# Mamba stage: where ScalarE's two silus, one evacuation and the norm's root, and VectorE's first two gates, stand in the loop body

## The chip, the cores and the metric

The kernel runs on one core of one Trainium2 chip, as one launch. The time is device time in microseconds (us) of that core. The program is written by hand for five queues: TensorE (PE), VectorE (DVE), ScalarE (ACT), GpSimd (POOL) and SyncE (SP, which only issues DMAs). Each runs its instructions in the order written, and they meet through semaphores.

## The reference

A chain of four blocks in float32 on x (8 x 512 x 256) and a context (8 x 64 x 192): attention with a feed-forward, a Mamba block, attention with a feed-forward, attention. The change touches the second, of which this is the core:

```
p = silu(prepend_cond @ pre_w1) @ pre_w2
h = concatenate([p, x], axis=1)
for l in range(4):
    h = h + mamba_block(rmsnorm(h, norm_w[l]), ...)

def mamba_block(x, ip_w, cw, cb, xp_w, dtp_w, dtp_b, A_log, Dp, op_w):
    xi, z = split(x @ ip_w.T)                  # 512 channels each
    xi = silu(conv(xi, cw, 4 taps, causal) + cb)
    dt, Bm, Cm = split(xi @ xp_w.T)            # 16, 16, 16
    dt = softplus(dt @ dtp_w.T + dtp_b)
    dA = exp(dt[..., None] * -exp(A_log))      # 512 channels x 16 states
    dBu = dt[..., None] * Bm[:, :, None, :] * xi[..., None]
    h_t = dA_t * h_(t-1) + dBu_t ;  ys_t = sum over states of h_t * C_t
    y = (ys + xi * Dp) * silu(z)
    return y @ op_w.T
```

With 8 batches of 64 + 512 positions there are 4608 positions a layer.

## The kernel before, in words

The Mamba stage (function `mamba`) cuts the 4608 positions of a layer into 9 chunks of 512 (`TC`) and walks layer by layer, chunk by chunk: 36 loop bodies, written out. The 512 channels x 16 states are 64 units of 128 rows (i = 0 to 63), two to a pair (j = i // 2, 0 to 31), and eight pairs to each fourth of the channels (k = j // 8).

For each unit ScalarE makes the decays, `exp(dt * A)`, into one of four banks of PSUM (line 2474); VectorE runs the scan along the 512 positions (line 2429); then the state is multiplied by C. In 22 of 32 pairs VectorE does that product (`times_c`, line 2237), in the ten pairs of `BY_POOL` (0, 5, 8, 11, 14, 16, 20, 24, 26, 28) GpSimd does (line 2511), three pairs behind its own product of u and B (line 2506), which fills a ring of six pairs. TensorE adds up each pair by two times two matmuls with `fold` into a bank for y (line 2384, `summed`). After eight pairs `gate` (line 2232) multiplies that bank by silu(z).

Before ScalarE makes the exponentials of pair j, `slots_free` waits until pair j-2 has left its banks. For a pair of VectorE it waits for the product (`prod_d`) and copies the last state out of the banks (line 2133); for a pair of GpSimd it waits for the scan (`scanned`) and copies from the ring (line 2129).

Between the exponentials the same body prepares the next chunk: the operations that are not the scan's are hung on an index. TensorE's projections stand at pairs, before the pair's own sum: convolution products E0 to E3 (line 1992; the last at pairs 2 and 3), the residual products B1 and B0 (lines 2034 and 2043; pairs 5 and 6), the norm's mean C (line 2018; pair 7), the products for dt, B and C, named G (line 2052; pairs 10 and 11), dt's products H and z's products F. ScalarE's evacuations stand behind the exponential of a unit: for each i, the exponential, then what `late_act` hangs on i, then what `early_act` hangs on i. `E_OUT` holds the units of the four convolution evacuations, `SILU_AT` those of silu of x and silu of z, each over 128 x 2048 with a table load before it and one behind it (lines 2173, 2174 and 2168, 2169). `RESIDUAL` is (19, 18): the evacuation of B0 (line 2143) behind unit 19, of B1 behind 18. `SQUARE_AT` is 5: a copy of three columns (line 2204) and the square (line 2205). `RSTD_AT` holds the logarithm (line 2208) and the exponential (line 2211) of the norm; VectorE applies the result at units 26 and 27 (line 2222). The gates of fourths 0, 1 and 2 stand before the scans 23, 39 and 55; that of fourth 3 before scan 7 of the next body.

The z of a body is given its silu in that body, the x of the next chunk in this one; G waits for the latter. GpSimd forms u = dt * x (`times_x`, line 2252), behind pairs 26 and 31, followed by one small operation (line 2255) which sets dt to a large value where a batch begins in the chunk, and otherwise writes to a scratch column. SyncE copies dt and u to all rows a fourth ahead (lines 2267 and 2274), stores B and C (line 2279), loads them again spread out, and loads the next layer's weights in the last two chunks of a layer.

Of the kernel before, what the change touches and what calls it, by code (L numbers as in the profile page):

```python
# [18 lines left out]
ALU = mybir.AluOpType  # L19
# [1804 lines left out]
def load_first(e, core, layer):  # L1824

    e.dma_start(core.weights[1][:, CONV_AT:CONV_AT + TAPS * KD * DI], layer_of(core.taps, layer)).then_inc(core.first_loaded, 16)
    e.dma_start(layer_vec(core, "norm", "conv_b"), vec_from(core, layer, "norm", "conv_b")).then_inc(core.first_loaded, 16)
# [62 lines left out]
def v_at(N, name):  # L1890

    return BEFORE_V[name] + 1 if N[1] == -2 else val(N, len(LANE_V), V_BASE + LANE_V[name] + 1)
# [17 lines left out]
def mamba(core):  # L1910
    at = 0
    ring, at = core.area(at, RING, 2, TC)
    dt_rep, at = core.area(at, 2, 2, TC)
    u_rep, at = core.area(at, 2, 2, TC)
    x, at = core.area(at, 2, KI, TC)
    z, at = core.area(at, 2, KI, TC)
# [61 lines left out]
    def reset_of(c):  # L1978

        return 64 * (c % CHUNKS) if c % CHUNKS < B else None  # L1980
# [125 lines left out]
            e.wait_ge(y_free, y_free_at(N, "F1"))  # L2106
        e.matmul(ybank[k % 2], diag[:, k, :], xi[:, k, :], start=True, stop=False)

    E_OUT, G_OUT, F_OUT, SILU_AT = (59, 3, 9, 13), 29, (55, 49, 33, 1), (15, 7)
    H_OUT = (37, 45)  # L2110

    def soft_plus(e, N, pair):
# [82 lines left out]
            e.wait_ge(ln.v_full, v_at(N, "F0"))  # L2195
            e.activation(zi[:, 0, :], lane_v, ACT.Copy).then_inc(ln.v_free, 1)

    SQUARE_AT, RSTD_AT, SCALE_AT = 5, (21, 23), 26

    def early_act(e, N, i, c, xe, nb, nb_before):  # L2200

# [45 lines left out]
    def times_x(e, N, pair, xi, c):  # L2247

        e.wait_ge(ln.s_free, s_at(N, ("H0", "H3")[pair]))
        e.wait_ge(ln.v_free, v_at(N, ("H1", "H2")[pair]))  # L2250
        at = slice(2 * pair, 2 * pair + 2)
        e.tensor_tensor(u[:, at, :], dt[:, at, :], xi[:, at, :], ALU.mult).then_inc(u_done, 1)
        e.wait_ge(u_done, u_done_at(N, pair, 1))
        p = reset_of(c)
        e.tensor_tensor(scrap[:, 12:14] if p is None else dt[:, at, p], far, core.one[:, 0:2], ALU.mult).then_inc(u_done, 1)

    def build_diag(e):

# [26 lines left out]
    with core.nc.Block() as block:  # L2285
        @block.sync
        def _(e):
            store_bc(e, (0, -1), 0)
            e.wait_ge(bc_stored, 16)
            for a in range(2):  # L2290
                for q in range(2):
                    load_bc(e, (0, -1), a, q, 0)
            e.wait_ge(u_done, u_done_at((0, -1), 0, 2))
            spread_dt(e, 0)
            spread_u(e, 0)
            for a in range(2, SP_):
                for q in range(2):
                    load_bc(e, (0, -1), a, q, 0)
            e.wait_ge(u_done, KI)
            for l in range(LAYERS // 2):  # L2300
                for j in range(BODIES):
                    N, c = (l, j), j % CHUNKS
                    layer = l * 2 + j // CHUNKS
                    after = (l * 2 + 2) % LAYERS if j >= CHUNKS else l * 2 + 1
                    e.wait_ge(summed, summed_at(previous(N), PAIRS_N - 1))
                    spread_dt(e, 1)
                    spread_u(e, 1)
                    if c == CHUNKS - 1:
                        load_z(e, core, after)
                    e.wait_ge(scanned, scanned_at(N, 15))  # L2310
                    spread_dt(e, 2)
                    spread_u(e, 2)
                    if c == CHUNKS - 2:
                        load_first(e, core, after)
                    store_bc(e, N, (j + 1) % 2)
                    e.wait_ge(scanned, scanned_at(N, 31))
                    spread_dt(e, 3)
                    e.wait_ge(bc_stored, val(N, 16, 32))
                    spread_u(e, 3)
                    if c == 0:  # L2320
                        load_out(e, core, layer)
                    e.wait_ge(u_done, u_done_at(N, 0, 2))
                    spread_u(e, 0)
                    e.wait_ge(scanned, scanned_at(N, 47))
                    spread_dt(e, 0)
                    if c == CHUNKS - 2:
                        load_middle(e, core, after)
                    for a in range(SP_):
                        pair = 3 * SP_ + a
                        if by_pool(pair):  # L2330
                            e.wait_ge(prod_q, prod_q_at(N, pair))
                        else:
                            e.wait_ge(prod_d, prod_d_at(N, pair))
                        load_bc(e, N, a, 0, (j + 1) % 2)
                        load_bc(e, N, a, 1, (j + 1) % 2)
            for a in range(SP_ // 2):
                e.wait_ge(bc_ready[a], 64 * (STEPS + 1))
            e.wait_ge(rep_in[0], 128 * (2 * STEPS + 1))
            e.wait_ge(rep_in[1], 128 * 2 * STEPS)
            e.wait_ge(core.first_loaded, FIRST_LOAD * (LAYERS + 1))  # L2340
            e.wait_ge(core.z_loaded, Z_LOAD * (LAYERS + 1))
            e.wait_ge(core.middle_loaded, MIDDLE_LOAD * (LAYERS + 1))
            e.wait_ge(core.out_loaded, OUT_LOAD * (LAYERS + 1))
# [49 lines left out]
        @block.vector  # L2393
        def _(e):
            e.memset(state, 0.0).then_inc(set_up, 1)
            e.memset(scrap[:, 18:22], 0.0)
            e.memset(far, FAR).then_inc(set_up, 1)
            e.memset(tiny, TINY).then_inc(set_up, 1)
            e.tensor_tensor(fold, core.ident[:, 0:64], core.ident[:, 64:128], ALU.add).then_inc(set_up, 1)
            e.memset(scrap[:, 1:2], 0.0).then_inc(prod_d, 1)  # L2400
            e.memset(scrap[:, 2:3], 0.0).then_inc(prod_d, 1)
            e.memset(scrap[:, 3:4], 0.0).then_inc(gated, 1)
            for i in range(RING - 1):
                e.memset(scrap[:, 4 + i:5 + i], 0.0).then_inc(summed, 1)
            e.wait_ge(core.first_loaded, FIRST_LOAD)
            for i in range(UN):
                early_dve(e, (0, -2), i, -2, normed[:, 0])
            for i in range(UN):
                early_dve(e, (0, -1), i, -1, normed[:, 1])
            for l in range(LAYERS // 2):  # L2410
                for n in range(BODIES):
                    N, c = (l, n), n % CHUNKS
                    layer = l * 2 + n // CHUNKS
                    for i in range(UN):
                        j, h = i // 2, i % 2
                        k, a = j // SP_, j % SP_
                        if c == CHUNKS - 2 and i == SCALE_AT:
                            e.wait_ge(core.first_loaded, layer * FIRST_LOAD + 2 * FIRST_LOAD)
                        early_dve(e, N, i, c, normed[:, n % 2])
                        for f in range(KI - 1):  # L2420
                            if i == 16 * (f + 1) + 7:
                                gate(e, N, f, z[:, n % 2])
                        if i == 7:
                            gate(e, previous(N), KI - 1, z[:, (n + 1) % 2])
                        if h == 0:
                            e.wait_ge(fed, fed_at(N, j))
                        e.wait_ge(da_full, da_full_at(N, i))
                        da, ub = banks[:, slot_of(i), :], ring_pair(n, j)[:, h, :]
                        e.tensor_tensor_scan(ub if by_pool(j) else da, da, ub, state[:, i:i + 1], ALU.mult, ALU.add).then_inc(scanned, 1)  # L2429
                        if h == 0 and j > 0 and not by_pool(j - 1):  # L2430
                            e.wait_ge(scanned, scanned_at(N, i - 1))
                            times_c(e, N, n, j - 1, 1)
                        if h == 1 and not by_pool(j):
                            e.wait_ge(scanned, scanned_at(N, i - 1))
                            times_c(e, N, n, j, 0)
                        if h == 1 and j == PAIRS_N - 1 and not by_pool(j):
                            e.wait_ge(scanned, scanned_at(N, i))
                            times_c(e, N, n, j, 1)
            N = (LAYERS // 2, 0)
            gate(e, previous(N), KI - 1, z[:, (BODIES - 1) % 2])  # L2440
            for m in range(KD):
                e.wait_ge((ln.s_full, ln.v_full)[m], (s_at(previous(N), "E2"), v_at(previous(N), "E1"))[m] + 1)
                xc = chunk(CHUNKS - 1)[:, m, :]
                e.tensor_tensor(xc, xc, lanes[1 - m], ALU.add)
# [384 lines left out]
```

## Time and profile before

| | us |
|---|---|
| median of 3 runs | 6636.77 |
| lowest and highest run | 6634.72, 6638.04 |
| the profiled execution, its own time | 6639.8 |
| its span | 6638.0 |
| VectorE busy over the span | 4928.1 |
| GpSimd busy over the span | 4394.1 |

The span is the time from the first to the last instruction that the profiler recorded; all times in rows are counted from its start. The mean granted clock of TensorE was 0.941 of its full speed. A row of a timeline is an instruction, or several of one kind behind each other (x2); the bracket at its end is the time for which its engine had stood idle before it, and what ended that. PE rows are matmuls, PEld rows weight loads. The Mamba stage's scans run from 2054.0 to 5992.7 us.

### The profile page before, as it was taken

Reading aid. Unit: us, or ns where it says so; the run is one execution under the profiler, and the core shown is the slowest. Engines: PE = TensorE matmul, PEld = TensorE weight load, DVE = VectorE, ACT = ScalarE, POOL = GpSimd, SP = SyncE. Lnnn points to the kernel's source line nnn. Section 1 sums busy time; section 2 is a strip of 40 time slices with the busy share of each in tenths; the row PEclk is TensorE's granted clock in tenths of the full one; section 3 lists DMA queues with packets and bytes.
Section 4 is the critical chain, followed back from the end, with each engine's and each line's share of the span. In section 5 each row is a group of like instructions: output and inputs, shape, how many; then the busy total and the mean of one; then the engine's idle time right before and its main releaser. Section 6 shows DMA issues by size and latency. Waiting matters only on the chain. (4 is left out here: it accounts for less than half of the span.)

```text
span 6638.0 us, 60681 instructions
## 1 busy us (share of the span) xinstructions
PE 6129.0 (92%) x20586; PEld 2577.4 (39%) x20586; DVE 4928.1 (74%) x5709; ACT 3620.5 (55%) x6605; POOL 4394.1 (66%) x2056
## 2 busy tenths in 40 slices
PE   9999999999999989898899989898989898988898
PEld 4555555544443333323333323333323343323444
DVE  4444445543225999999999999999999999995623
ACT  4444445432225666666666666666666666664432
POOL 3333334323005999999999999999999999992300
PEclk9999999999998989899989999999999898989998
DMA  2000000213002333333333333332333232332000
GB/s 80 1 1 1 1 1 1 86 26 102 20 0 68 83 76 78 78 93 85 72 89 71 83 88 86 71 89 65 89 81 93 65 89 65 93 80 56 4 0 26
DMA packets 228678, 387.64 MB, mean 58 GB/s; under 512 B 46304, under 2 KB 64416, under 8 KB 225936
## 3 DMA queue, kind: packets, MB, share of 16 engines
q1 hardware_dynamic: 228368, 383.75, 23.7%
q8 instruction: 164, 2.69, 0.2%
q14 instruction: 146, 1.20, 0.1%
HBM read 207.14 MB, written 23.40 MB: 35 GB/s over the span
## 5 line engine op out<-in xcount | busy, mean ns | idle before, releaser
L2506 POOL TENSOR_TENSOR work<-work,weights 128x1024 f32<-128x1024 f32 x1152 | 2685.6, 2361 | 15.8 <-PE banks L2384 6.8
L2429 DVE TENSOR_TENSOR_SCAN banks<-banks,work 128x512 f32<-128x512 f32 x1584 | 1985.7, 1272 | 53.5 <-ACT banks L2474 48.1
L2384 PE MATMUL banks<-work 128*64 128x512 f32 x4608 | 1353.9, 670 | 378.2 <-POOL work L2511 271.1
L2474 ACT ACTIVATE banks<-work 128x512 f32<-128x512 f32 x2304 | 1496.0, 680 | 25.5
L1992 PE MATMUL banks<-work,weights 128*128 128x512 f32 (+31 forms) x3796 | 1140.6, 451 | 3.0 <-DVE work L2222 3.0
L2237 DVE TENSOR_TENSOR work<-banks,weights 128x512 f32<-128x512 f32 x1584 | 1056.0, 668 | 0.0
L2511 POOL TENSOR_TENSOR work<-work,weights 128x1024 f32<-128x1024 f32 x360 | 848.0, 2356 | 238.4 <-ACT work L2129 238.4
L2429 DVE TENSOR_TENSOR_SCAN work<-banks,work 128x512 f32<-128x512 f32 x720 | 911.2, 1269 | 99.8 <-ACT banks L2474 97.2
L603 POOL TENSOR_TENSOR work<-work 128x1024 f32<-128x1024 f32 x256 | 479.6, 1893 | 743.4 <-DVE work L470 742.9
L1992 PEld LDWEIGHTS banks<-work,weights 128*128 128x128 f32 x3796 | 634.4, 190 | 600.0 <-issue 523.6
L2133 ACT ACTIVATE work<-banks 128x2 f32<-128x2 f32 x792 | 135.9, 172 | 1227.4 <-DVE work L2237 1225.6
L2384 PEld LDWEIGHTS banks<-work 128*64 128x64 f32 x4608 | 271.0, 145 | 1236.4 <-issue 500.8
L553 ACT ACTIVATE work<-banks,work 128x512 f32<-128x512 f32 x512 | 347.7, 690 | 201.1 <-DVE work L464 201.1
L464 DVE TENSOR_REDUCE work<-banks 128x2 f32<-128x1024 f32 x256 | 308.8, 1214 | 105.1 <-PE banks L389 104.7
L2010 PE MATMUL banks<-work,weights 128*128 128x512 f32 x592 | 350.7, 722 | 0.0
L1040 PE MATMUL banks<-work,weights 128*128 128x512 f32 x768 | 341.5, 599 | 9.4 <-ACT work L215 9.4
L454 DVE COPY work<-banks 128x512 f32<-128x512 f32 x256 | 175.5, 685 | 160.3 <-PE banks L379 160.3
L379 PE MATMUL banks<-ident,work 128*128 128x128 f32 x2048 | 277.9, 279 | 8.2 <-DVE work L454 4.6
L379 PEld LDWEIGHTS banks<-ident,work 128*128 128x128 f32 x2048 | 222.1, 141 | 151.7 <-issue 111.1
L389 PE MATMUL banks<-work 64*128 64x512 f32 x1024 | 254.4, 615 | 0.0
L366 PE MATMUL banks<-work 128*64 128x256 f32 x2048 | 247.5, 385 | 0.0
L322 PE MATMUL banks<-work,weights 128*128 128x512 f32 x512 | 224.9, 597 | 6.4 <-ACT work L215 4.2
(312 smaller groups left out, 6796.9 us busy)
## 6 DMA issues: line engine op xcount, KB each, us to landing
weights<-mamba_bc SPq DMA_DIRECT2D x592, 256.0 KB, 5.0
work<-work SPq DMA_DIRECT2D x1160, 128.0 KB, 2.3
weights<-mamba_taps SPq DMA_DIRECT2D x5, 2048.0 KB, 7.5
weights<-cross_vo SPq DMA_DIRECT2D x16, 512.0 KB, 6.9
mamba_taps<-work SPq DMA_DIRECT2D x4, 2048.0 KB, 7.8
cross_vo<-weights SPq DMA_DIRECT2D x6, 1024.0 KB, 8.4
work<-in_conv_rows SPq DMA_DIRECT2D x16, 256.0 KB, 6.7
out_T<-X SPq DMA_DIRECT2D x8, 512.0 KB, 3.3
```

Source lines behind the costliest of these rows:

```text
L379: mm = e.transpose(core.banks[:, 4 + j, kt * P:(kt + 1) * P], probs[:, 2 * (g % 2) + u, j, kt * P:(kt + 1) * P], core.ident[:])
L553: last = e.activation(probs[:, slot, j, :], core.banks[:, 2 * u + j, :], ACT.Exp, bias=nmax[:, slot, j:j + 1], accum_out=sums[:, slot, j:j ...
L603: e.tensor_tensor(probs[:, slot], probs[:, slot], rsum[:, slot, :].unsqueeze(2).to_broadcast([P, 2, T]), ALU.mult) \
L1040: mm = e.matmul(bank(i), w1[:, k, m * P:(m + 1) * P], normed[:, k, :], start=(k == 0), stop=(k == KD - 1))
L1992: mm = e.matmul(lane[:, a:b], conv_w[j][:, k, m * P:(m + 1) * P], nb[:, k, a + j:b + j], start=(d == 0 and k == 0), stop=(j == 0 and b == ...
L2010: mm = e.matmul(lane, z_w[:, k, m * P:(m + 1) * P], nb[:, k, TAPS - 1:], start=(k == 0), stop=(k == KD - 1))
L2237: last = e.tensor_tensor(ring_pair(n, j)[:, h, :], banks[:, slot_of(i), :], bc[:, j % SP_, 1, :], ALU.mult)
L2384: mm = e.matmul(ybank[k % 2][64 * h:64 * h + 64, :], fold, ring_pair(n, j)[:, h, :], start=False, stop=(a == SP_ - 1))
L2429: e.tensor_tensor_scan(ub if by_pool(j) else da, da, ub, state[:, i:i + 1], ALU.mult, ALU.add).then_inc(scanned, 1)
L2474: e.activation(banks[:, slot_of(i), :], dt_rep[:, k % 2, h, :], ACT.Exp, scale=decay[:, f:f + 1]).then_inc(da_full, 1)
L2506: e.tensor_tensor(ring_pair(n, j), u_rep[:, k % 2], bc[:, a, 0, :].unsqueeze(1).to_broadcast([P, 2, TC]), ALU.mult) \
L2511: e.tensor_tensor(ring_pair(n, q), ring_pair(n, q), bc[:, q % SP_, 1, :].unsqueeze(1).to_broadcast([P, 2, TC]), ALU.mult) \
```

## The change

Four indices move, one small operation and one semaphore step of GpSimd go, and SyncE gets a wait.

- `E_OUT[3]`: the last convolution evacuation stands behind unit 15 in place of 13.
- `SILU_AT`: silu of x behind unit 21 (pair 10) in place of 15, silu of z behind unit 5 (pair 2) in place of 7. At unit 5 `late_act`, with the silu, comes ahead of `early_act`, with the square.
- `RSTD_AT`: logarithm and exponential behind units 23 and 24 in place of 21 and 23.
- `GATE_AT`: the first two gates before scans 21 and 37 in place of 23 and 39; the third stays at 55.
- `times_x`: in a chunk in which no batch begins (the last of each layer) the second operation is left out, and the first counts for two.
- SyncE waits for the last convolution evacuation before it loads the next layer's folded convolution weights.

```diff
--- before.py
+++ after.py
@@ -2106,7 +2106,9 @@
             e.wait_ge(y_free, y_free_at(N, "F1"))
         e.matmul(ybank[k % 2], diag[:, k, :], xi[:, k, :], start=True, stop=False)
 
-    E_OUT, G_OUT, F_OUT, SILU_AT = (59, 3, 9, 13), 29, (55, 49, 33, 1), (15, 7)
+    E_OUT, G_OUT, F_OUT = (59, 3, 9, 15), 29, (55, 49, 33, 1)
+    SILU_AT = (21, 5)
+    GATE_AT = (21, 37, 55)
     H_OUT = (37, 45)
 
     def soft_plus(e, N, pair):
@@ -2195,7 +2197,7 @@
             e.wait_ge(ln.v_full, v_at(N, "F0"))
             e.activation(zi[:, 0, :], lane_v, ACT.Copy).then_inc(ln.v_free, 1)
 
-    SQUARE_AT, RSTD_AT, SCALE_AT = 5, (21, 23), 26
+    SQUARE_AT, RSTD_AT, SCALE_AT = 5, (23, 24), 26
 
     def early_act(e, N, i, c, xe, nb, nb_before):
 
@@ -2249,10 +2251,12 @@
         e.wait_ge(ln.s_free, s_at(N, ("H0", "H3")[pair]))
         e.wait_ge(ln.v_free, v_at(N, ("H1", "H2")[pair]))
         at = slice(2 * pair, 2 * pair + 2)
-        e.tensor_tensor(u[:, at, :], dt[:, at, :], xi[:, at, :], ALU.mult).then_inc(u_done, 1)
+        p = reset_of(c)
+        e.tensor_tensor(u[:, at, :], dt[:, at, :], xi[:, at, :], ALU.mult).then_inc(u_done, 2 if p is None else 1)
+        if p is None:
+            return
         e.wait_ge(u_done, u_done_at(N, pair, 1))
-        p = reset_of(c)
-        e.tensor_tensor(scrap[:, 12:14] if p is None else dt[:, at, p], far, core.one[:, 0:2], ALU.mult).then_inc(u_done, 1)
+        e.tensor_tensor(dt[:, at, p], far, core.one[:, 0:2], ALU.mult).then_inc(u_done, 1)
 
     def build_diag(e):
 
@@ -2311,6 +2315,7 @@
                     spread_dt(e, 2)
                     spread_u(e, 2)
                     if c == CHUNKS - 2:
+                        e.wait_ge(ln.v_free, v_at(N, "E3"))
                         load_first(e, core, after)
                     store_bc(e, N, (j + 1) % 2)
                     e.wait_ge(scanned, scanned_at(N, 31))
@@ -2418,7 +2423,7 @@
                             e.wait_ge(core.first_loaded, layer * FIRST_LOAD + 2 * FIRST_LOAD)
                         early_dve(e, N, i, c, normed[:, n % 2])
                         for f in range(KI - 1):
-                            if i == 16 * (f + 1) + 7:
+                            if i == GATE_AT[f]:
                                 gate(e, N, f, z[:, n % 2])
                         if i == 7:
                             gate(e, previous(N), KI - 1, z[:, (n + 1) % 2])
```

## Rows read from the trace of the kernel before

**Rows 1.** The page: busy table (us, share of the span); ScalarE's exponentials (busy us, mean ns of one).

```profile
PE 6129.0 (92%) x20586; PEld 2577.4 (39%) x20586; DVE 4928.1 (74%) x5709; ACT 3620.5 (55%) x6605; POOL 4394.1 (66%) x2056
...
L2474 ACT ACTIVATE banks<-work 128x512 f32<-128x512 f32 x2304 | 1496.0, 680 | 25.5
```

**Rows 2.** Waits of 2000 to 6200 us: who waited for whom, us, times, longest.

```profile
POOL work L2511 <- ACT work L2129: 238.4, 145, 7.1
...
DVE work L2429 <- ACT banks L2474: 97.2, 37, 25.8
...
DVE banks L2429 <- ACT banks L2474: 48.1, 41, 6.4
...
ACT X L2143 <- PE banks L2043: 16.2, 36, 0.5
DVE work L2232 <- PE banks L2384: 16.2, 8, 12.1
```

**Rows 3.** Windows: PE, PEld, DVE, ACT, POOL busy us (x), PEclk, DMA, GB/s.

```profile
3482.11:3591.08 108.97, 99.46 (x306) 38.17 (x305) 105.79 (x115) 70.39 (x127) 102.41 (x47) 0.91 0.34 78
3482.11:3514.00 31.89, 31.89 (x113) 15.16 (x111) 28.83 (x32) 24.35 (x38) 27.72 (x12) 1.00 0.40 89
3536.00:3544.00 8.00, 7.97 (x16) 1.90 (x18) 8.00 (x10) 6.10 (x10) 8.00 (x4) 0.61 0.60 131
```

**Rows 4.** Timeline of VectorE, one body: start, us, engine, line, op, out<-in [idle].

```profile
3479.94 2.44 DVE L2429 TENSOR_TENSOR_SCAN work<-banks,work 128x512 f32<-128x512 f32 x2
...
3488.80 1.27 DVE L2429 TENSOR_TENSOR_SCAN banks<-banks,work 128x512 f32<-128x512 f32 x1
...
3494.17 1.29 DVE L2429 TENSOR_TENSOR_SCAN banks<-banks,work 128x512 f32<-128x512 f32 x1 [1.14 <-ACT banks L2474]
...
3509.20 1.28 DVE L2429 TENSOR_TENSOR_SCAN work<-banks,work 128x512 f32<-128x512 f32 x1 [1.92 <-ACT banks L2474]
...
3518.66 1.27 DVE L2429 TENSOR_TENSOR_SCAN work<-banks,work 128x512 f32<-128x512 f32 x1
3519.85 0.66 DVE L2237 TENSOR_TENSOR work<-banks,weights 128x512 f32<-128x512 f32 x1
3520.43 0.68 DVE L2232 TENSOR_TENSOR work<-banks,work 128x512 f32<-128x512 f32 x1
3521.03 1.27 DVE L2429 TENSOR_TENSOR_SCAN work<-banks,work 128x512 f32<-128x512 f32 x1
...
3545.53 1.29 DVE L2429 TENSOR_TENSOR_SCAN banks<-banks,work 128x512 f32<-128x512 f32 x1
```

**Rows 5.** Timeline of ScalarE in the same body.

```profile
3484.10 1.04 ACT L2205 ACTIVATE work<-X 128x1024 f32<-128x1024 f32 x1
3487.13 0.17 ACT L2133 ACTIVATE work<-banks 128x2 f32<-128x2 f32 x1 [2.00 <-DVE work L2237]
...
3488.66 1.28 ACT L2168 ACT_TABLE_LOAD   x1
...
3493.17 0.17 ACT L2133 ACTIVATE work<-banks 128x2 f32<-128x2 f32 x1
3493.38 1.30 ACT L2474 ACTIVATE banks<-work 128x512 f32<-128x512 f32 x2
...
3513.54 0.60 ACT L2143 ACTIVATE X<-banks 128x512 f32<-128x512 f32 x1 [0.46 <-PE banks L2043]
...
3514.13 1.29 ACT L2474 ACTIVATE banks<-work 128x512 f32<-128x512 f32 x2
```

**Rows 6.** Timeline of TensorE in the same body.

```profile
3509.91 3.60 PE L2043 MATMUL banks<-work,weights 128*128 128x512 f32 x8
...
3516.36 1.08 PE L2384 MATMUL banks<-work 128*64 128x512 f32 x4
...
3540.00 1.98 PE L2384 MATMUL banks<-work 128*64 128x512 f32 x4
```

**Rows 7.** The GpSimd operation of line 2255: ns min/median/max, first and last start.

```profile
L2255 POOL TENSOR_TENSOR work<-work,one x74: 196/197/198, 2038.7 to 5992.3; 128x2 f32<-128x2 f32 x74
```

## The prediction

> **What bounds the kernel now.** I read, in this order, the busy table of the page, the waits over the Mamba stage, one body of that stage in the windows, and then that body instruction by instruction on VectorE, ScalarE, TensorE and GpSimd. The busy table puts TensorE first [rows 1], but that is a mean over eight stages, and the change touches only the Mamba stage. There the loop body runs 36 times, and one body takes 108.97 us, in which VectorE is busy 105.79, GpSimd 102.41, TensorE 99.46 and ScalarE 70.39 [rows 3]. VectorE, with its 64 scans and 44 products by C, is therefore the bound, and it is idle for only 3.2 us a body. The waits say where: scans wait for ScalarE's exponentials, 97.2 + 48.1 us in all [rows 2], of which one wait of 25.8 is the prologue's. The gates lost only 16.2 us to TensorE over the whole stage, 12.1 of them in one wait at the end. GpSimd's 238.4 us are spent waiting for copies of the state, which come behind VectorE's own scans: slack, not a bound.
>
> In the body read here the idle time of VectorE is two waits: 1.14 us before scan 8, and 1.92 us before scan 16 [rows 4]. Each follows a silu on ScalarE. A silu costs a table load, the activation and a second load: from 3488.66 to 3493.17, that is 4.51 us [rows 5]. The exponentials run at most two pairs ahead, since four banks hold them, so such a block is hidden only if ScalarE's lead is long enough. The next op of VectorE follows a scan after 1.19 us and a product or gate after 0.59 (scan 22, product, gate and scan 23 at 3518.66, 3519.85, 3520.43 and 3521.03) [rows 4]. Without its waits, scan 8 would have started 1.22 earlier and scan 16 2.00 earlier; with about 0.13 before scan 38 [rows 4] the body loses 3.35 us, or 120 us in 36 bodies. That is all that any new order on ScalarE could win.
>
> All times below are of the body whose first scan is at 3479.9, in the span's clock. I carry the new order through it with these durations: copy to first exponential 0.20, one exponential 0.68 [rows 1], a pair of them 1.30, and 0.11 from its end to the scan that waited for it (3493.17, 3493.38 + 0.68, 3494.17) [rows 4, 5].
>
> **Silu of z behind pair 2 (i = 5).** At i = 5 ScalarE is free at 3484.0; what stood there was the square, a small copy and 1.04 us [rows 5]. Pair 3 could start at 3487.13, when its slot came free, so ScalarE had 3 us left over, of which the square took 1.1. Now the silu goes ahead of the square in the same step: 3484.05 + 4.53 = 3488.58, square to 3489.7, copy, exponential 6 done at 3489.7 + 0.20 + 0.68 = 3490.6, scan 6 at 3490.7. It started at 3488.80 before [rows 4]: 1.90 us lost in place of 1.22. By scan 8 VectorE is 0.68 behind the old time. The silu has not become hidden; it has met the square.
>
> **The convolution's last evacuation at i = 15, silu of x no longer there.** The evacuation behind exponential 15 costs no one anything: the next user of its lane is the mean product, much later, and the exponentials 16 and 17 wait for a slot anyway. With no silu, scan 16 goes at the old 3509.20 - 2.00 + 0.68 = 3507.9. VectorE is now 1.3 us ahead of the old time. This is the whole gain, and it stands for about four scans.
>
> **What is late next: TensorE's residual product.** At i = 19 ScalarE evacuates the product of line 2043. Its eight matmuls run from 3509.91 to 3513.51, and ScalarE waited 0.46 for them at 3513.54 [rows 5, 6]; it did so 36 times for 16.2 us [rows 2], so in every body. TensorE is busy without a gap from the body's start to here, 31.89 of 31.89 us at clock 1.00 [rows 3], so this product can't come sooner because VectorE does: its time is fixed to the body's start. ScalarE, 1.3 us earlier at i = 19, only waits longer. It takes up pair 10 at 3514.03 as before and its exponentials at 3514.13 [rows 5]; the first is done at 3514.81 and scan 20 starts at 3514.92. VectorE would have been ready at 3513.8 (from scan 16 four scans at 1.19 and two products at 0.59: 5.9). That is a new wait of 1.1 us, and the gain is spent: the old scan 20 stood two scans and two products, 3.56, ahead of scan 22's 3518.66 [rows 4], at 3515.1.
>
> **Silu of x behind pair 10 (i = 21).** The exponentials 20 and 21 end at 3515.42. The silu follows, to 3519.95; copy and exponential 22: 3519.95 + 0.20 + 0.68 + 0.11 = scan 22 at 3520.94. Before, it started at 3518.66 [rows 4]. **The gate moved to i = 21** stands ahead of scan 21 and needs pair 7's sum, whose four matmuls end at 3517.44 [rows 6]: it waits some 0.7 us, scan 21 starts at 3518.1 and scan 22 could start at 3519.9. So this wait lies wholly under the one for the exponential. The gate that stood before scan 23 is gone there; scan 23 starts at 3520.94 + 1.19 + 0.59 = 3522.72, where it was 3521.03 [rows 4]: **1.69 us late**, and from there on everything that follows VectorE is late by as much.
>
> **The rest.** The logarithm and exponential of the norm at i = 23 and 24 lie in ScalarE's slack: exponential 24 is done at 3523.7 for a scan that can start at 3523.9, exponential 25 at 3524.8 for one at 3525.1, and the scale step at i = 26 finds its input. The two margins are 0.1 us; if both fail, 0.3 us a body more. The gate moved from i = 39 to 37 needs the sum of pair 15, whose matmuls end at 3541.98 [rows 6], for a gate due at about 3543.6: free, and as it is now ahead of scan 38, the 0.13 lost there [rows 4] goes. The operation left out in the product of dt and x is 0.20 us of GpSimd [rows 7] twice a layer, 8 times: below 2 us of an engine with slack, nothing. GpSimd takes up its product by C for pair 11 about 1.5 us later, behind the copy of pair 11's state, and TensorE's sum of pair 11 comes after; both are shifted with VectorE and not beyond it. SyncE's new wait, four times, is for an evacuation at i = 15 and stands behind a wait for scan 15 and the copies of pair 16's operands, and ahead of a store that waits for i = 29: it is over when reached. Nothing: between 0 and 1 us each, were it not.
>
> **The sum.** 1.69 - 0.13 = 1.56 us a body, times 36 = +56 us. The profiled execution's own time is 6639.8 us (span 6638.0), 3.0 over the median of the runs, 6636.77. 6639.8 + 56 = 6696; put on the median, 6693 us. Bounds of the sum by body: if scan 22's lateness were 0.3 less (the evacuation found ready by its 0.46) 1.26, if the two margins fail 1.86: 6682 to 6704.
>
> One rule of the Trainium skill speaks of what this does to TensorE. The row first: while TensorE works without gaps the granted clock is 1.00 (2.4 GHz), and in a stretch that follows gaps it is 0.61 in the mean, between the two levels; a pair's four matmuls take 1.08 us in the one and 1.98 in the other [rows 3, 6]. The page "TensorE: Matmul & The Clock Gate", section "Part 1: The HAM clock gate (the "warmup" mystery)", says that the slow level is the default, to which TensorE falls back when it has been idle. By that rule a longer gap in mid-body, about 1.5 us more before pair 11's sum, can bring more slow matmuls; in the sum above they fall where TensorE waits for others anyway, so the rule leaves 6693 as it is; where they reached the residual product, the time would be the third rival's, 6729 or more.
>
> **Rivals.**
> 1. *Both silus are hidden and every wait of VectorE goes.* This is the other side: 3.35 x 36 = -120 us, 6517. For it: VectorE's 105.79 of 108.97, and a state copied right behind a scan (pairs 0 and 8) gives the slot sooner. Against it: by the rows ScalarE has 3.8 us between 3484.05 and the last moment for pair 3's copy, 3487.85, and puts 5.6 into it. It decides at scan 6: were it at 3488.8, this is it. 4%.
> 2. *The residual product is there when ScalarE asks* (TensorE ahead of where this trace has it). Then pair 10's exponentials start at 3512.3, the silu ends at 3518.1, scan 22 is at 3519.1 and scan 23 at 3520.9, 0.15 early; with scan 38's 0.13, -0.28 x 36 = -10 us, 6627. Against it: 36 waits of 36, and TensorE without a gap. 7%.
> 3. *TensorE is slower where it sets the time.* If the residual product's eight matmuls fell into a slow stretch, 3.60 x 1.98 / 1.08 = 6.6, +3.0 us in such a body; in a third of the bodies +36, 6729, in all +108, 6801. For it: a body of a new length. Against it: no gap ahead of that run in the rows. 9%.
> 4. *Only the z side shows*: the x side breaks even, 0.68 - 0.13 = 0.55 x 36 = +20, 6657. 5%.
>
> **How the numbers follow.** The forecast has 75%: 6693. The range is 6650 to 6718: the forecast with its bounds, the fourth rival, and a small part of the third. About 0.2% (13 us) is what a measurement of this kernel can tell from no change. Slower by more: the forecast, the third and fourth rivals less a little, 0.87. Within: most of the second and a tail of the fourth, 0.07. Faster: the first and the rest of the second, 0.06.
>
> **What would show it.** In the changed profile: the body at 110.5 us; a wait of about 1.8 us before scan 6 and none before scan 8; none before scan 16; about 1.1 before scan 20; a gate waiting some 0.7 for TensorE before scan 21; about 1 before scan 22; and ScalarE's wait for line 2043's product grown from 0.46 to some 1.8 us a body. The total of scans waiting for exponentials should be about 4 us a body. It is wrong if scan 20 doesn't wait, or if the residual product ends sooner than 33.6 us behind the body's first scan.

## The result, and the profile after

The changed kernel takes 6686.32 us (median of 4 runs, 6685.67 to 6688.22), the kernel before 6637.02 beside it: +49.3 us, a ratio of 1.0075 with a 95% interval of 1.0061 to 1.009. It is slower, as forecast (6693, range 6650 to 6718). The profiled execution has a span of 6684.2 us, 46.2 over the one before.

The waits of the Mamba stage in the changed kernel, in the columns of [rows 2]. Line numbers have moved: the scan is L2434, the exponentials L2479, the residual evacuation L2145, the gate L2234.

```profile
POOL work L2516 <- ACT work L2131: 277.0, 180, 6.2
...
DVE banks L2434 <- ACT banks L2479: 116.3, 71, 6.4
...
ACT X L2145 <- PE banks L2043: 73.3, 36, 3.2
...
DVE work L2434 <- ACT banks L2479: 58.5, 37, 22.5
...
DVE work L2234 <- PE banks L2389: 36.3, 37, 11.8
```

Scans wait 174.8 us for exponentials (145.3 before), the gates 36.3 us for TensorE (16.2), and ScalarE waits 73.3 us for the residual product (16.2), still 36 times. Without the one long wait of the prologue (22.5 us, 25.8 before) the scans wait 152.3 us, 4.2 a body, where it was 119.5. One body of it, in the columns of [rows 3], then VectorE in the same body; it answers to [rows 4].

```profile
3495.15:3605.69 110.54, 97.95 (x305) 37.80 (x304) 105.90 (x115) 70.23 (x125) 102.49 (x47) 0.92 0.33 77
```

```profile
3495.15 2.44 DVE L2434 TENSOR_TENSOR_SCAN work<-banks,work 128x512 f32<-128x512 f32 x2
...
3505.85 1.29 DVE L2434 TENSOR_TENSOR_SCAN banks<-banks,work 128x512 f32<-128x512 f32 x1 [1.77 <-ACT banks L2479]
...
3523.03 1.27 DVE L2434 TENSOR_TENSOR_SCAN work<-banks,work 128x512 f32<-128x512 f32 x1
...
3530.13 1.29 DVE L2434 TENSOR_TENSOR_SCAN banks<-banks,work 128x512 f32<-128x512 f32 x1 [1.11 <-ACT banks L2479]
...
3532.70 0.69 DVE L2234 TENSOR_TENSOR work<-banks,work 128x512 f32<-128x512 f32 x1 [0.70 <-PE banks L2389]
...
3536.17 1.28 DVE L2434 TENSOR_TENSOR_SCAN work<-banks,work 128x512 f32<-128x512 f32 x1 [1.00 <-ACT banks L2479]
3537.37 0.67 DVE L2239 TENSOR_TENSOR work<-banks,weights 128x512 f32<-128x512 f32 x1
3537.95 1.27 DVE L2434 TENSOR_TENSOR_SCAN work<-banks,work 128x512 f32<-128x512 f32 x1
```

VectorE's busy time is the same to 0.1 us (105.90, 105.79 before [rows 3]); the body is 110.54 in place of 108.97, and the difference is idle. There are four waits where there were two: scan 6, scan 20, the gate ahead of scan 21, scan 22. Together they are 4.58 us (1.77 + 1.11 + 0.70 + 1.00) of the 4.64 in which VectorE is idle. Scan 16, at 3523.03, has no wait any more; it starts 27.88 us behind the body's first scan, where it was 29.26. Scan 23 starts 42.80 us behind the body's first scan (3537.95 - 3495.15); before it was 41.09. ScalarE and TensorE in that body, for [rows 5] and [rows 6]:

```profile
3499.29 1.28 ACT L2170 ACT_TABLE_LOAD   x1
3500.59 1.91 ACT L2170 ACTIVATE work<-work 128x2048 f32<-128x2048 f32 x1
3502.52 1.28 ACT L2171 ACT_TABLE_LOAD   x1
...
3503.93 1.04 ACT L2207 ACTIVATE work<-X 128x1024 f32<-128x1024 f32 x1
3504.87 0.15 ACT L2135 ACTIVATE work<-banks 128x2 f32<-128x2 f32 x1
3505.06 1.30 ACT L2479 ACTIVATE banks<-work 128x512 f32<-128x512 f32 x2
...
3528.76 0.60 ACT L2145 ACTIVATE X<-banks 128x512 f32<-128x512 f32 x1 [1.84 <-PE banks L2043]
...
3530.66 1.28 ACT L2175 ACT_TABLE_LOAD   x1
```

```profile
3525.12 3.60 PE L2043 MATMUL banks<-work,weights 128*128 128x512 f32 x8
...
3531.57 1.08 PE L2389 MATMUL banks<-work 128*64 128x512 f32 x4
```

The residual product ends at 3528.72, 33.57 us behind the body's first scan. Before it was 3513.51 - 3479.94 = 33.57. ScalarE came earlier and waited longer for it (1.84 in place of 0.46). The square stands between the silu of z and the copy of pair 3, with no gap on either side.

Where the 46.2 us of span are (starts of first scans, 36 bodies each):

| part | before | after | difference |
|---|---|---|---|
| ahead of the stage's first table load | 1981.8 | 1979.9 | -1.9 |
| prologue, to the first scan | 72.25 | 69.17 | -3.1 |
| first scan to the last gate | 3953.2 | 4009.0 | +55.8 |
| last gate to the next stage's table load | 60.1 | 61.3 | +1.2 |
| the stages behind | 570.7 | 564.8 | -5.9 |

The mean body (last first scan less the first, over 35) went from 109.49 to 111.06 us, +1.564; the forecast was +1.56. Most single bodies went from 108.9 to 110.5; the longer ones grew by 1.3 to 2.0.

### The profile page after: what moved, and what is told of

Same layout as the page of the kernel before. It is cut to its first block and busy times, and to the rows that moved or that the text cites. A ratio compares the mean times of both kernels' runs of the same rounds, so it can differ in the third digit from the quotient of the medians.

```text
span 6684.2 us, 60673 instructions
## 1 busy us (share of the span) xinstructions
PE 6131.0 (92%) x20586; PEld 2565.2 (38%) x20586; DVE 4932.7 (74%) x5709; ACT 3615.8 (54%) x6605; POOL 4397.2 (66%) x2048
## 5 line engine op out<-in xcount | busy, mean ns | idle before, releaser
L2434 DVE TENSOR_TENSOR_SCAN banks<-banks,work 128x512 f32<-128x512 f32 x1584 | 1986.6, 1272 | 121.8 <-ACT banks L2479 116.3
L2389 PE MATMUL banks<-work 128*64 128x512 f32 x4608 | 1324.9, 669 | 427.7 <-POOL work L2516 285.5
L2479 ACT ACTIVATE banks<-work 128x512 f32<-128x512 f32 x2304 | 1498.3, 680 | 25.5
L2434 DVE TENSOR_TENSOR_SCAN work<-banks,work 128x512 f32<-128x512 f32 x720 | 911.6, 1270 | 61.1 <-ACT banks L2479 58.5
```

The costliest lines, as they stand in the source:

```text
L2389: mm = e.matmul(ybank[k % 2][64 * h:64 * h + 64, :], fold, ring_pair(n, j)[:, h, :], start=False, stop=(a == SP_ - 1))
L2479: e.activation(banks[:, slot_of(i), :], dt_rep[:, k % 2, h, :], ACT.Exp, scale=decay[:, f:f + 1]).then_inc(da_full, 1)
```

## The experiments

All were timed in five rounds, each beside the kernel before on the same chip. The chips were three (z_only to gates_only on one, the last two rows on another, the rest on the third), so kernels of different groups are compared by their ratios. "Body" is the mean body, from the first scans of the profiled execution.

| run | us | ratio to before, 95% | body |
|---|---|---|---|
| before | 6638 to 6639 | | 109.49 |
| after_again | 6684.78 | 1.0070 (1.0057 to 1.0084) | 111.04 |
| z_only | 6640.77 | 1.0001 (0.9992 to 1.0010) | 109.54 |
| x_only | 6688.92 | 1.0072 (1.0060 to 1.0085) | 111.04 |
| e3_only | 6630.69 | 0.9988 (0.9979 to 0.9997) | 109.32 |
| gates_only | 6654.53 | 1.0024 (1.0015 to 1.0033) | 109.96 |
| resid_22 | 6651.36 | 1.0022 (1.0013 to 1.0031) | 109.94 |
| resid_22_gate_23 | 6618.72 | 0.9972 (0.9961 to 0.9982) | 109.03 |
| best | 6592.72 | 0.9932 (0.9920 to 0.9944) | 108.33 |
| best_resid_19 | 6626.41 | 0.9984 (0.9975 to 0.9993) | 109.21 |
| best_x21 | 6586.26 | 0.9922 (0.9909 to 0.9936) | 108.04 |

**Do the waits add, or are they tied to TensorE?** The theory of the prediction says that a scan behind an evacuation of a TensorE product has its time from the body's start, so that a delay or a gain ahead of it vanishes. Its rival is that each silu has a price of its own.

z_only, the kernel before with one number changed:

```diff
-    E_OUT, G_OUT, F_OUT, SILU_AT = (59, 3, 9, 13), 29, (55, 49, 33, 1), (15, 7)
+    E_OUT, G_OUT, F_OUT, SILU_AT = (59, 3, 9, 13), 29, (55, 49, 33, 1), (15, 5)
```

> The kernel before with silu of z behind unit 5 and nothing else. Theory (the scans are tied to TensorE's products at fixed times of the body): the wait moves from scan 8 to scan 6 and grows from 1.22 to 1.9 us, so VectorE is 0.68 late, but ScalarE's evacuation of the last convolution product waited 0.56 us for TensorE anyway and stays where it is, so scan 16 starts when it did, with its wait shrunk from 1.9 to 1.3 us. Body 108.97, time 6637 (no change). Rival (each silu's wait adds by itself): +0.68 x 36 = +24, 6661.

No change (1.0001). VectorE's waits of one body, whose first scan is at 3481.23:

```profile
3491.94 1.29 DVE L2429 TENSOR_TENSOR_SCAN banks<-banks,work 128x512 f32<-128x512 f32 x1 [1.76 <-ACT banks L2474]
...
3510.49 1.28 DVE L2429 TENSOR_TENSOR_SCAN work<-banks,work 128x512 f32<-128x512 f32 x1 [1.29 <-ACT banks L2474]
```

Scan 16 is at 29.26 us of the body in both (3510.49 - 3481.23, 3509.20 - 3479.94): the 0.6 us lost at scan 6 came back there. The product that ties scan 16 is not the residual one but the last convolution product: ScalarE waited 0.56 us for it before, here it doesn't wait, and silu of x starts 23.74 us into the body in both (3504.97 - 3481.23, 3503.68 - 3479.94). By itself the move of the silu of z costs nothing.

x_only, the changed kernel with the z side undone:

```diff
-    SILU_AT = (21, 5)
+    SILU_AT = (21, 7)
```

> The changed kernel with silu of z back behind unit 7; silu of x at 21, the evacuation at 15, the norm's root and the gates stay changed. Theory: the time of scan 22 is set by TensorE's residual product and the silu of x behind it, so the 0.68 us that VectorE wins at scan 8 is lost again in a longer wait before scan 20; body 110.5 as in the changed kernel, 6686. Rival (waits add): 24 us less, 6662.

6688.92, the changed kernel's time. The waits of one body:

```profile
3510.28 1.29 DVE L2434 TENSOR_TENSOR_SCAN banks<-banks,work 128x512 f32<-128x512 f32 x1 [1.14 <-ACT banks L2479]
...
3531.03 1.29 DVE L2434 TENSOR_TENSOR_SCAN banks<-banks,work 128x512 f32<-128x512 f32 x1 [1.74 <-ACT banks L2479]
```

What was won at the z side (1.14 in place of 1.77) was paid before scan 20 (1.74 in place of 1.11). So the rest of the change makes the whole loss without the move of the silu of z, and neither silu's wait adds to the other's. This run keeps the evacuation at 15, the norm's root and the sooner gates, so it doesn't single out the silu of x.

e3_only, the evacuation alone (with SyncE's wait, as in the change):

```diff
-    E_OUT, G_OUT, F_OUT, SILU_AT = (59, 3, 9, 13), 29, (55, 49, 33, 1), (15, 7)
+    E_OUT, G_OUT, F_OUT, SILU_AT = (59, 3, 9, 15), 29, (55, 49, 33, 1), (15, 7)
```

> The kernel before with only the last convolution evacuation moved from unit 13 to 15 (with SyncE's wait). Theory: exponentials 14 and 15 no longer wait for TensorE's convolution product, silu of x starts 0.60 us sooner and scan 16 too, but the residual product's evacuation at unit 19 still ends at the same time, so scan 20 gains only 0.19 us: -0.19 x 36 = -7, 6630. Rival (the residual product binds nothing): the whole 0.60 stays, -22, 6615.

6630.69, -0.12%: this part of the change was good by itself. Its body shows the wait of scan 16 down from 1.92 to 1.31 us and a new one of 0.31 before scan 20, the residual product's, which takes most of the gain (the body is 0.17 shorter for 0.19 forecast):

```profile
3505.09 1.28 DVE L2430 TENSOR_TENSOR_SCAN work<-banks,work 128x512 f32<-128x512 f32 x1 [1.31 <-ACT banks L2475]
...
3511.40 1.29 DVE L2430 TENSOR_TENSOR_SCAN banks<-banks,work 128x512 f32<-128x512 f32 x1 [0.31 <-ACT banks L2475]
```

gates_only, the kernel before with the gates at 21, 37 and 55:

```diff
-                            if i == 16 * (f + 1) + 7:
+                            if i == (21, 37, 55)[f]:
```

> The kernel before with only the gates moved to scans 21 and 37. Theory: the gate before scan 21 waits about 0.6 us for pair 7's sum, with no wait for an exponential to lie under, and the small loss of 0.13 before scan 38 goes: +0.49 x 36 = +18, 6655. Rival (two gates sooner are free, as under the changed kernel's wait): -0.13 x 36 = -5, 6632.

6654.53, +0.24%: with no wait for an exponential to lie under, the sooner gate costs. In the ordinary body of the trace it waits 0.51 us for pair 7's sum.

**Is it the residual product?** resid_22, the changed kernel with the evacuation moved behind the silu of x:

```diff
-    RESIDUAL = (19, 18)
+    RESIDUAL = (22, 18)
```

> The changed kernel with the residual product's evacuation (of TensorE line 2043) moved from unit 19 to 22, behind silu of x. Theory: the exponentials 20 and 21 come 2.4 us sooner, silu of x ends at 3517.6 in place of 3519.95, and what binds next is the gate before scan 21, which waits for pair 7's sum: scan 23 is 0.62 us later than before the change in place of 1.69. With scan 38's 0.13 that is +0.49 x 36 = +18 over the kernel before, 6657, some 31 us under the changed kernel. Rival (the silu itself is the whole cost, not TensorE's product ahead of it): no change against the changed kernel, 6687.

6651.36: one number takes back 33 us of after_again's 46, beside it on the same chip. In the loop it is more, 40 of the 55.8 us; the stages behind Mamba took 7.5 us longer in this run than in the changed kernel (below). The body's 109.94 is +0.45 on before for +0.49 forecast. The wait that is left is the gate's, and no scan waits between 6 and 23 (VectorE of one body):

```profile
3522.19 0.69 DVE L2234 TENSOR_TENSOR work<-banks,work 128x512 f32<-128x512 f32 x1 [1.91 <-PE banks L2389]
```

resid_22_gate_23, the same with `GATE_AT = (23, 37, 55)`:

> The same with the first gate back before scan 23. Theory: nothing of TensorE is waited for ahead of scan 22; it is set by silu of x alone, at 3518.6, where the kernel before had 3518.66: -0.19 x 36 = -7 against the kernel before, 6632. Rival (the gate's wait lies under the silu's, as in the changed kernel): as the run without it, 6657.

6618.72, 13 us better than expected. The ordinary body is 108.7 (108.9 before), as expected. Some 9 us of surplus come from seven longer bodies, the seventh of each layer and the first of layers 2 to 4, which gained 1.3 to 1.6 us each; 6 more come from the stages behind Mamba (564.6 us in place of 570.7), and smaller differences elsewhere take 2 back. In the longer bodies TensorE's run is longer (the residual product ends 35.5 us behind the first scan in the body at 3697.92), and that body went from 110.8 to 109.3. I had taken all 36 bodies as one. The trace of the kernel before shows which product sets the time there: ScalarE waits 2.31 us for the last convolution product at unit 13, and scans 14 and 16 wait behind it.

```profile
3721.55 0.69 ACT L2161 ACTIVATE work<-banks,weights 128x512 f32<-128x512 f32 x1 [2.31 <-PE banks L1992]
...
3723.01 1.29 DVE L2429 TENSOR_TENSOR_SCAN banks<-banks,work 128x512 f32<-128x512 f32 x1 [1.19 <-ACT banks L2474]
...
3729.06 1.28 DVE L2429 TENSOR_TENSOR_SCAN work<-banks,work 128x512 f32<-128x512 f32 x1 [2.39 <-ACT banks L2474]
```

resid_22_gate_23 has that evacuation at 15, silu of x at 21 and the residual evacuation at 22, and only two waits are left in this body, 2.33 us before scan 6 and 1.18 before scan 22. With fewer of the three moves more is left: e3_only made the body 110.5, since it lost what it won in a wait of 1.01 us before scan 20, and best (below), with silu of x at 15, keeps a wait of 2.21 us before scan 16.

**A version that beats both.** best, from the kernel before:

```diff
-    E_OUT, G_OUT, F_OUT, SILU_AT = (59, 3, 9, 13), 29, (55, 49, 33, 1), (15, 7)
+    E_OUT, G_OUT, F_OUT, SILU_AT = (59, 3, 9, 15), 29, (55, 49, 33, 1), (15, 5)
...
-    RESIDUAL = (19, 18)
+    RESIDUAL = (22, 18)
...
-    SQUARE_AT, RSTD_AT, SCALE_AT = 5, (21, 23), 26
+    SQUARE_AT, RSTD_AT, SCALE_AT = 11, (23, 24), 26
...
+                        e.wait_ge(ln.v_free, v_at(N, "E3"))
                         load_first(e, core, after)
...
-                            if i == 16 * (f + 1) + 7:
+                            if i == (23, 37, 55)[f]:
```

> From the kernel before: silu of z behind unit 5 but the square moved to 11, last convolution evacuation at 15, silu of x left at 15, residual evacuation at 22, the norm's root at 23 and 24, gates before scans 23, 37 and 55. Theory: the wait at scan 6 is 0.8 us (1.22 before at scan 8), that at scan 16 is 1.3 to 1.4 (2.00 before), and with nothing tied to TensorE ahead of scan 23 both gains are kept: -(0.45 + 0.64 + 0.13) = -1.22 x 36 = -44, 6595. Rival (another product of TensorE clips it, the mean or pair 7's sum): -0.3 x 36, 6628.

6592.72, -0.68%. Its two waits of a body, before scans 6 and 16:

```profile
3476.47 1.29 DVE L2430 TENSOR_TENSOR_SCAN banks<-banks,work 128x512 f32<-128x512 f32 x1 [0.71 <-ACT banks L2475]
...
3495.04 1.28 DVE L2430 TENSOR_TENSOR_SCAN work<-banks,work 128x512 f32<-128x512 f32 x1 [1.32 <-ACT banks L2475]
```

With the square out of the way the silu of z behind pair 2 is the better place (0.71 against 1.14 before). best_resid_19 puts only `RESIDUAL` back to (19, 18):

> The version that beat both kernels, with the residual product's evacuation back behind unit 19, where both kernels had it. Theory: what is won at scans 6 and 16 (1.09 us) is lost again in a wait before scan 20, which can't start before 33.6 us of the body plus the evacuation, copy and exponential (35.0 behind scan 0); left are 0.19 and scan 38's 0.13: -0.32 x 36 = -12 against the kernel before, 6627. Rival (the other moves of that version, not this one, made its gain): as the version itself, 6593.

6626.41: 33 of best's 46 us are gone (each against the kernel before beside it), through one wait before scan 20:

```profile
3512.80 1.29 DVE L2430 TENSOR_TENSOR_SCAN banks<-banks,work 128x512 f32<-128x512 f32 x1 [0.74 <-ACT banks L2475]
```

That scan is at 34.96 us of its body (first scan 3477.84), the changed kernel's at 34.98 (3530.13 - 3495.15), x_only's at 35.00 (3531.03 - 3496.03), e3_only's at 34.97 (3511.40 - 3476.43). These four have the residual evacuation behind unit 19 and differ in where silu of z, silu of x or the square stand ahead of it, and the scan has one time. best_x21 is best with `SILU_AT` (21, 5), as the change has it:

> The version that beat both kernels, with silu of x behind unit 21, where the change put it, in place of 15. Theory: with the evacuation at 22 and the square at 11 that place is as good as 15: scan 16 starts without a wait, silu of x ends at about 3516.5, scan 22 starts at 3517.5 where the kernel before had 3518.66; -(1.16 + 0.13) x 36 = -46, 6592, and perhaps 8 less for the bodies near a layer's end, which gained more than the others when the same was done to the changed kernel. Rival (unit 21 is itself a bad place for the silu): slower than that version by some 1 us a body, 6630.

6586.26, the lowest time: two waits a body, of 0.70 us before scan 6 and 1.18 before scan 22. The intervals of its ratio and best's overlap, but its mean body is 0.29 us shorter.

```profile
3473.16 1.29 DVE L2430 TENSOR_TENSOR_SCAN banks<-banks,work 128x512 f32<-128x512 f32 x1 [0.70 <-ACT banks L2475]
...
3501.06 1.28 DVE L2430 TENSOR_TENSOR_SCAN work<-banks,work 128x512 f32<-128x512 f32 x1 [1.18 <-ACT banks L2475]
```

So both places that the change chose for the silus are good ones, once the square, the residual evacuation and the first gate are out of their way.

**What of the time is not the change's?** after_again:

> The changed kernel once more, to see how much of its time outside the loop bodies is the run's own spread: the body stays at 110.5 us; the prologue's 3 us stay if they come from the order there (the residual evacuations ahead of silu of x); the 6 us by which the stages behind Mamba were shorter stay only if they are the change's. Time 6687.

6684.78, body 111.04, prologue 67.7 us; the stages behind took 564.8 us again. Over all traces these stages, with the same code, take one of two lengths: 564.6 to 566.2 us in the changed kernel (twice), x_only, resid_22_gate_23, best, best_resid_19 and best_x21, and 570.7 to 572.5 in the kernel before, z_only, e3_only, gates_only and resid_22. Between the changed kernel and the one before, 4 to 5 of the 6 us arise near the end, where TensorE's granted clock differs. The stretch from 55 to 40 us before the end, in the kernel before and then in the changed one, in the columns of [rows 3]:

```profile
6583.00:6598.00 15.00, 12.47 (x58) 11.07 (x60) 4.64 (x7) 3.76 (x6) 2.94 (x2) 0.60 0.11 40
```

```profile
6629.20:6644.20 15.00, 13.33 (x68) 8.66 (x68) 8.59 (x13) 3.76 (x6) 2.94 (x2) 0.84 0.19 71
```

The clock is 0.60 in the one, with 58 matmuls done, and 0.84 in the other, with 68. The slow stretch doesn't always lie there: best has 0.58 in it, but 1.00 in the 10 us before, where the kernel before has 0.69. What in a kernel decides which of them it gets stays open.

## Why the prediction was right

- *The z side*: 1.90 us late at scan 6 forecast; the trace has an idle time of 1.77 and a start 1.84 later than without a wait (3505.85, where the product at 3503.42 plus 0.59 gives 3504.01). The square's part is confirmed by best: with the square at 11 that wait is 0.71, 1.06 less, and the square took 1.04.
- *Gain at scan 16*: no wait left and 1.3 us sooner forecast; there is none (3523.03), and it is 1.38 sooner in the body. The prediction put the old wait there down to silu of x alone; e3_only shows that 0.6 us of it were the last convolution product's (1.92 to 1.31). The change takes both away, so the sum didn't suffer.
- *The residual product fixed to the body's start*: 33.57 us in both, and in the longer body at 3697.92 and its match at 3716.30 it ends at 35.45 in both. This was the step that turned the sign. Waits before scan 20, gate and scan 22 forecast at 1.1, 0.7 and about 1 us, measured 1.11, 0.70 and 1.00. ScalarE's wait 1.84 for 1.8.
- *Lateness at scan 23*: 1.71 for 1.69. The two margins of 0.1 us at exponentials 24 and 25 held: no scan waits there.
- *The gate at 37 and scan 38*: no wait in the profile; the body is 1.57 longer, not 1.71.
- *The terms put at nothing*: the norm's root and GpSimd's small operation were not run alone. The four waits account for 4.58 of the body's 4.64 idle us, which leaves next to nothing for them.
- *The sum*: +55.8 in the loop for +56. So close a match is in part luck: the sum took all bodies as one, and single bodies grew by 1.3 to 2.0 us. Outside the loop the sum had nothing, and the two profiles differ by -9.7 us there: -5.9 in the stages behind, which the runs tie to no part of the change (resid_22 differs from the changed kernel in one number and took 572.3 there), -3.1 in the prologue, -1.9 ahead of the stage, +1.2 behind the last gate. They put the result, 6686, under the forecast: by 7 us and not 10, since the medians differ by 3 us more than the two profiles.

The prologue's waits of TensorE, before and then after. Columns as in [rows 6]:

```profile
2025.69 5.33 PE L2052 MATMUL banks<-work,weights 128*48 128x512 f32 x8 [2.78 <-ACT work L2143]
```

```profile
2022.64 3.61 PE L2052 MATMUL banks<-work,weights 128*48 128x512 f32 x8 [1.45 <-ACT work L2175]
```

Before, the product G waited for its bank until the residual evacuation, queued behind silu of x and its second table load; after, the evacuation is ahead of the silu, and G waits for the silu alone. The stage began 1.9 us earlier in that run, so G starts 1.15 sooner in the stage, and its eight matmuls take 3.61 in place of 5.33 us. The changed kernel, after_again and x_only, which share this order, have a prologue of 69.2, 67.7 and 69.1 us; z_only has 70.6, and the other eight kernels have 72.0 to 72.3.

- *The rivals.* The first (all waits hidden) failed where the prediction put its decision, at scan 6. The second (the product ready when asked) is refuted by 36 waits of 36. The fourth (only the z side shows) is the wrong way round: x_only shows all, z_only nothing. The third, TensorE's clock, can be read in two places. The body's granted clock is 0.92 (0.91 before), so the longer body brought no slow stretch to the residual product, which took 3.60 us again. In the prologue of the kernel before, TensorE stood idle for 2.78 us, and the eight matmuls behind ran at a granted clock of 0.68 in the mean, between the two levels (5.33 us); in the changed kernel it stood idle for 1.45, and they ran at 1.00 (3.61 us). The Trainium skill's page "TensorE: Matmul & The Clock Gate" (section "Part 1: The HAM clock gate (the "warmup" mystery)") says that the slow level is the default and follows idleness; these two traces agree with it. But the gap alone doesn't decide: of the nine kernels with a gap of 2.78 us, eight took 5.0 to 5.3 us for G, and z_only took 3.63 at a clock of 1.00:

```profile
2027.17 3.63 PE L2052 MATMUL banks<-work,weights 128*48 128x512 f32 x8 [2.78 <-ACT work L2143]
```

So of the prologue's 3.1 us only the sooner start is the order's for certain; the 1.7 us of faster matmuls need the clock to stay up as well.

## What to carry to other kernels

Take an engine that isn't the bound but feeds the one that is, and works through a queue in fixed order. Before you move an instruction in it, look for instructions ahead of its new place that wait for a third engine. If that engine runs without a gap up to its product, as TensorE did here (31.89 of 31.89 us), the product has a fixed time in the body, and what is won ahead of it is lost at it, but for the slack that was there (0.17 us of 0.6 stayed in e3_only).

A short wait in every iteration (0.46 us, 36 of 36) on such an engine is the sign. Here moving that evacuation was worth 33 us together with the other moves. No run moves it alone in the kernel before, where no scan waited for it.

Count a moved instruction together with all that shares its slot: the square cost 1.06 us at scan 6, more than the 0.43 that the better place of the silu gives (0.71 in place of 1.14).

## What was not expected

The effects of single moves don't add. Silu of z at 5 is worth nothing in the kernel before (1.0001), the last convolution evacuation at 15 is worth -8 us, and best_x21 -53 us (6586.26 against 6638.96): it has these two and silu of x at 21, with the square, the norm's root, the residual evacuation and the second gate moved too. The stages behind Mamba take either about 565 or about 571 us in kernels with the same code there, a difference as large as some of the effects measured here.
